# Moving split work, the row norms and the expert offsets of layer 0, and taking layer 1's row norm as factors

## The chip, the cores and the metric

The kernel runs on one core of a Trainium2 chip. The metric is device time in microseconds (us) of one execution. TensorE multiplies matrices, VectorE and ScalarE work on rows and on PSUM results, POOL (GpSimd) prepares the weights, and SyncE issues the DMA transfers. TensorE's granted clock has two levels, 1.2 and 2.4 GHz; the profile writes it as a share of full speed.

## The reference

One graph of 1250 nodes (512 values each) and 20000 edges goes through four layers. What the change touches is the end of layer 0's mixer, layer 0's experts, and layer 1:

```
# layer 0, depth i of 2 (end of it)
y = layernorm(x); h = gelu(y @ W1[i] + b1[i]); x = x + h @ W2[i] + b2[i]
# layer 0, experts, on xf = layernorm(x): two of eight by gate
y = einsum('te,teh->th', combine, relu(xf @ w1 + b1) @ w2 + b2)   # b2: the offsets
x = x + y + relu(xf @ sw1 + sb1) @ sw2 + sb2                      # shared expert
# layer 1, on xn = layernorm(x)
h = (segment_sum(xn[src], dst) / count) @ W_l.T + b_l + xn @ W_r.T
gnn = relu(batchnorm_over_nodes(h)) + xn
z = xn / max(norm(xn), 1e-12) * norm_w * sqrt(512)                # row norm
q, k, v = split(z @ w_qkv); q = softmax over head dims, k = softmax over nodes
x = x + gnn + rmsnorm(attention(q, k, v) @ w_out + b_out)
```

## The kernel before

The 1250 rows are ten tiles t of 125 rows, in three chunks CH of 4, 4 and 2 tiles; the 512 columns are four groups k of 128. A product takes the activations transposed, as a pair of 16-bit halves (high and low), and the weights likewise as a pair, in three passes: `gemm_N` (line 498) gives rows in ten PSUM banks of 12 matmuls, `gemm_T` (line 480) gives transposed results in twelve banks of 12 matmuls, eight of 500 columns and four of 250. PSUM has three rings: "act" (three banks, emptied by ScalarE), "dve" (three, emptied by VectorE) and "both" (two).

**Weights.** A unit is one 512x512 weight. There are two unit slots in SBUF. SyncE loads a unit in four quarters through two raw slots; POOL makes each quarter into its halves with three instructions (`split_quarter`: scale at line 2655, high half at 2657, low half at 2659). POOL and SyncE go through the units u in order, written out by hand: before unit u, POOL waits until the product that used unit u-2 has ended; after it come `4 * SPLIT_AFTER[u]` quarters of the later layers' expert weights, which go by four staging slots in `AT` back to memory. After the last of these (`max(SPLIT_AFTER)`, unit 25) SyncE waits for all stores and loads the adjacency, 3.1 MB, back into `AT` (lines 2883 to 2885). Only then does it issue the quarters of the next unit. SyncE also loads bias rows into two slots, and each waits there for its slot.

Units: 0 is layer 0's graph product; 1 to 12 and 13 to 24 are the two depths of the mixer (4 and 16 are the output products, 5 to 12 and 17 to 24 the hidden layer, in four blocks b of `gemm_T` and `gemm_N`); 25 to 28 the eight experts, 29 and 30 the shared expert; 31 and 32 layer 1's W_l and W_r, both used by one product (`bnT`); 33, 34, 35, 36 its q, k, v and output weights.

**Ends of the depths.** In the last block (b = 3) VectorE takes each tile from PSUM into `M` (line 1850), adds the bias row (1853), in depth 1 adds `M` to `X` (2140), and takes the statistics (1793). At depth 0 the norm, the transposes and the halves of the next product (`normed_columns`, `split_columns`) run beside the last tiles; at depth 1 ScalarE's `ln_root(Y)` norms the rows, and TensorE transposes them (line 430), after the last product. Each act bank of transposes is free again when VectorE has made its low half (1837). The first expert product is interrupted after three banks by the gate's logits.

**Offsets.** `expert_biases` transposes the gates (8 rows) and multiplies them with the 32-bit offset rows E0, 8x512, tile by tile (line 885). VectorE adds each result to `X`; then it adds the experts' results (2375), one instruction for a tile of three matmuls.

**Layer 1.** `gather_N("agg")` sums neighbours (line 539, ten tiles; `AT` has to be back), and in its steps dt the transposes of `M` and of the sums are interleaved (1090), copied by ScalarE (1351) and halved by VectorE. After `bnT` VectorE takes the batch statistics over all banks (2409), ScalarE applies them (1656), VectorE adds `M` to `X` (2424), TensorE transposes back (457) and VectorE adds that (1850). ScalarE squares the rows of `M` (1694), VectorE scales them into `Y` (2526), and TensorE transposes them (430); ScalarE and VectorE make the halves. Then `linear_attention(1)`: q product, query softmax on VectorE (2436 to 2452) with ScalarE's exp, transposes of q, k product (ScalarE empties it), column maxima of k (2458), v product.

## Time and profile before

| | |
|---|---|
| median of 3 runs | 3175.11 us (3169.66 to 3175.34) |
| the profiled execution | 3171.26 us, span 3169.5 us |
| TensorE busy | 2704.7 us (85%), granted clock 0.921 |
| VectorE busy | 1708.1 us (54%) |
| ScalarE, POOL busy | 1125.9 us (36%), 1193.4 us (38%) |

Busy time is that of the whole span. A row of a timeline gives start and length in us, the engine, the line, the operation with the shapes out<-in, the count of instructions merged into it, and in brackets the idle time ahead of it with what ended it. In the numbers of matmuls some records may be missing.

### The profile page before, as it was taken

How to read it: one execution, taken by the hardware profiler on the slowest of the kernel's cores; microseconds unless marked ns; L12 is line 12 of the kernel's file. 1: busy time of each engine (PE TensorE's matmuls, PEld its weight loads, DVE VectorE, ACT ScalarE, POOL GpSimd, SP SyncE). 2: the span in 40 equal slices, each digit the busy share in tenths (PEclk: the TensorE clock that was granted, in tenths of full speed). 3: DMA queues.
4: the chain of work that ended last, by engine and by line, in shares of the span. 5: the costliest groups of instructions: out<-in, count | busy, mean ns of one | idle time of the engine just before them, and what ended most of it. 6: DMA issues, size and time to landing. Idle time of an engine off the chain costs nothing. (4 is left out here: it accounts for less than half of the span.)

```text
span 3169.5 us, 46348 instructions
## 1 busy us (share of the span) xinstructions
PE 2704.7 (85%) x17011; PEld 1760.6 (56%) x17011; DVE 1708.1 (54%) x3454; ACT 1125.9 (36%) x2510; POOL 1193.4 (38%) x1445
## 2 busy tenths in 40 slices
PE   8999899799889889899986956999599958589784
PEld 4655668456558646455544635777355645355453
DVE  8875878434678833655527253222435466541543
ACT  3254466233447522313214323444332235320132
POOL 2031677885377788623212212111003226300042
PEclk9999899999999999989997977999799979798887
DMA  2011445442154444411100007999601059600198
GB/s 63 1 51 37 126 144 160 139 130 80 47 153 147 153 134 131 136 33 34 37 11 27 31 15 286 416 417 414 200 4 38 21 210 322 211 14 0 33 365 271
DMA packets 163941, 415.35 MB, mean 131 GB/s; under 512 B 23931, under 2 KB 75675, under 8 KB 140236
## 3 DMA queue, kind: packets, MB, share of 16 engines
q1 hardware_dynamic: 149213, 362.10, 33.6%
q0 software_dynamic: 12960, 42.48, 3.5%
q10 hardware_dynamic: 1555, 7.95, 1.0%
q8 instruction: 132, 2.16, 0.3%
q14 instruction: 81, 0.66, 0.1%
HBM read 325.37 MB, written 87.09 MB: 130 GB/s over the span
## 5 line engine op out<-in xcount | busy, mean ns | idle before, releaser
L2655 POOL TENSOR_SCALAR raw<-raw 128x512 f32<-128x512 f32 x380 | 271.6, 715 | 1085.8 <-PE ps L480 434.7
L498 PE MATMUL ps<-units,ARENA 128*125 128x512 f16 x2880 | 643.9, 385 | 35.0 <-POOL units L2659 25.6
L480 PE MATMUL ps<-ARENA,units 128*128 128x500 f16 (+1 forms) x2952 | 537.5, 344 | 19.6 <-ACT tmp L1415 9.4
L498 PEld LDWEIGHTS ps<-units,ARENA 128*125 128x125 f16 x2880 | 391.1, 138 | 274.6 <-POOL units L2659 26.1
L480 PEld LDWEIGHTS ps<-ARENA,units 128*128 128x128 f16 x2952 | 289.2, 98 | 265.6 <-issue 19.0
L1813 DVE TENSOR_TENSOR ARENA<-tmp,ARENA 128x500 f16<-128x500 f32 (+3 forms) x241 | 173.1, 723 | 360.8 <-ACT ARENA L1341 187.6
L2659 POOL TENSOR_TENSOR AT<-raw,AT 128x512 f16<-128x512 f32 x200 | 243.9, 1220 | 17.0
L1340 ACT ACTIVATE tmp<-ps,cols 128x500 f32<-128x500 f32 (+1 forms) x156 | 95.7, 613 | 395.1 <-PE ps L480 385.3
L2703 POOL DMA_INDIRECT ARENA<-rows_d,proj x81 | 80.0, 987 | 389.0 <-DVE ARENA L2200 363.0
L2659 POOL TENSOR_TENSOR units<-raw,units 128x512 f16<-128x512 f32 x180 | 217.6, 1209 | 15.3
L2708 POOL DMA_INDIRECT picks_d<-ARENA,proj x81 | 82.1, 1014 | 345.1 <-DVE ARENA L2240 344.5
L973 PE MATMUL ps<-ARENA 128*128 128x128 f16 x3240 | 191.7, 220 | 0.1
L973 PEld LDWEIGHTS ps<-ARENA 128*128 128x128 f16 x3240 | 187.4, 98 | 1.5 <-DVE ARENA L2231 0.6
L988 PE MATMUL ps<-ARENA 128*128 128x512 f16 x810 | 184.2, 380 | 0.0
L1850 DVE SCALAR_TENSOR_TENSOR ARENA<-ps,ARENA 125x512 f32<-125x512 f32 x100 | 68.7, 687 | 153.6 <-PE ps L498 153.4
L430 PE MATMUL ps<-ident,ARENA 125*128 125x125 f32 x280 | 53.1, 352 | 111.8 <-DVE ARENA L1837 33.5
L1594 ACT ACTIVATE tmp<-ps,proj 128x128 f32<-128x128 f32 x270 | 102.6, 380 | 102.8 <-PE ps L973 72.7
L2657 POOL CAST AT<-raw 128x512 f16<-128x512 f32 x200 | 132.9, 664 | 12.8
L613 PE MATMUL ps<-ARENA 125*125 125x500 f16 (+1 forms) x588 | 118.6, 353 | 10.9 <-DVE ARENA L1915 9.9
L988 PEld LDWEIGHTS ps<-ARENA 128*128 128x128 f16 x810 | 74.8, 98 | 95.1 <-issue 12.2
L2240 DVE TENSOR_SCALAR ARENA<-ps,proj 128x512 f32<-128x512 f32 x81 | 60.7, 750 | 121.0 <-PE ps L988 76.9
L655 PE MATMUL ps<-proj,ARENA 128*125 128x256 f16 x640 | 106.0, 296 | 22.3 <-ACT AT L1526 11.4
(445 smaller groups left out, 4578.2 us busy)
## 6 DMA issues: line engine op xcount, KB each, us to landing
ARENA<-split_d SPq DMA_DIRECT2D x135, 1024.0 KB, 11.6
raw<-in_moe SPq DMA_DIRECT2D x200, 256.0 KB, 3.0
split_d<-AT SPq DMA_DIRECT2D x200, 256.0 KB, 2.5
raw<-in_units SPq DMA_DIRECT2D x180, 256.0 KB, 2.5
ARENA<-split_d SPq DMA_DIRECT2D x27, 1280.0 KB, 8.9
rows_d<-ARENA SPq DMA_DIRECT2D x6, 896.0 KB
ARENA<-picks_d SPq DMA_DIRECT2D x6, 896.0 KB
ARENA<-picks_d ACTq DMA_DIRECT2D x6, 896.0 KB
```

Source lines behind the costliest of these rows:

```text
L480: ins = pe.matmul(o[:, 0:nt * R], wt, mv_, start=(i == 0), stop=(i == len(steps) - 1))
L498: ins = pe.matmul(o[0:R, :], th(srcT, h, k, t, 1), w(k, g), start=(i == 0), stop=(i == len(steps) - 1))
L613: ins = pe.matmul(psA[b][0:R, 0:a1 - a0], ohd[j][:, 0:R], ohs[j][:, a0:a1], start=False, stop=False)
L655: ins = pe.matmul(o[0:R, h2 * NBF:(h2 + 1) * NBF], stack(2 * hp + h2, t, 1), features(dep, part), start=(part == 0), stop=(part == 1))
L973: ins = pe.matmul(o[:, oc * B:(oc + 1) * B], w1[:, gw, kk, oc * 128:(oc + 1) * 128], tile_T[g % 2][:, h, kk, :], start=(i == 0), stop=(i = ...
L988: ins = pe.matmul(o[:, :], tile_H[(g - 1) % 2][:, h, b * KC + kk, :], w2[:, gw, kk, :], start=False, stop=(b == halves - 1 and i == len(st ...
L1340: act.activation(tmp[:, i % STAGES, 0:width], o[:, 0:width], func, bias=bias, scale=scale)
L1594: act.activation(tmp[:, i % STAGES, oc * B:(oc + 1) * B], o[:, oc * B:(oc + 1) * B], func, bias=bias, scale=WS)
L1813: tt(lo, tmp[:, staged[0] % STAGES, 0:width], hi, ALU.subtract).then_inc(sem("lo_T"), s.one("lo_T"))
L2655: pool.tensor_scalar(r, r, WEIGHT_SCALE, 1.0, ALU.mult, ALU.mult).then_inc(sem("pool_step"), 1)
L2657: pool.tensor_copy(hi, r).then_inc(sem("pool_step"), 1)
L2659: pool.tensor_tensor(lo, r, hi, ALU.subtract).then_inc(sem(name), 1)
```

## The change

- `SPLIT_AFTER`: units 4, 5, 16, 17 are followed by 32 quarters of expert weights instead of 36; units 26, 27, 28, 29 by 4 each instead of none. The adjacency comes back after unit 29 instead of 25.
- Last blocks of both depths: the bias row is added in block 2 (and in depth 1 `M` is then added to `X`); block 3 adds its products directly to `M` (depth 0) or `X` (depth 1), followed by the statistics alone.
- Depth 1's row norm: the first chunk's transposes go ahead of tile 8 of the last product, the second's and third's behind it, with the copies and low halves interleaved on ScalarE and VectorE.
- Offsets: gates and offsets as 16-bit parts, stacked in 72 rows (high at 0 and 32/64, low), so each tile is one 72x512 16-bit matmul. New copies on VectorE (`offsets_in_parts`, and four instructions in `gates`).
- Layer 1: `M`'s squares are taken by ScalarE at the start of the gather; the norm becomes a factor per row, `row_scale`, applied in q's exp and in v's evacuation, and as a row vector over the columns (`token_scale`, from ten small matmuls with `ones`) in k's evacuation, which VectorE now does. `L1nw` is folded into units 33 to 35 by POOL. The q, k, v products read the transposed `xn` that `bnT` used. `bnT` goes to `M` in transposed form, its statistics are taken bank by bank, its affine step runs between q's exps, and its transposes come after k and q's transposes. The sums X + M move into the gather's steps.

```diff
-SPLIT_AFTER = {4: 9, 5: 9, 16: 9, 17: 9}
-SPLIT_AFTER.update({u: 1 for u in [6, 7, 8, 9, 10, 11] + [18, 19, 20, 21, 22, 23, 24, 25]})
+SPLIT_AFTER = {4: 8, 5: 8, 16: 8, 17: 8}
+SPLIT_AFTER.update({u: 1 for u in [6, 7, 8, 9, 10, 11] + [18, 19, 20, 21, 22, 23, 24, 25, 26, 27, 28, 29]})
...
 # TensorE
+            def direct_columns(c):
+                t0, nt = CH[c]
+                pe.wait_ge(sem("normed"), s.more("normed", nt))
+                for k in range(KC):
+                    pe.wait_ge(*left("act"))
+                    o = bank("act", "lo_D")
...
+            def beside_direct(t):
+                if t == 8:
+                    direct_columns(0)
...
-                    pe.matmul(o[0:R, :], combT[:, t * R:(t + 1) * R], row_slots[0:8, ROWS.index(row) % ROW_SLOTS, :], start=True, stop=True).then_inc(sem("filled_dve"), 1)
+                    pe.matmul(o[0:R, :], combT[:, t * R:(t + 1) * R], offset16[:, :], start=True, stop=True).then_inc(sem("filled_dve"), 1)
...
-            transposes_T(lambda t, a, b: nat(Y, t, a, b), "normed", "lo_D")
+            direct_columns(1)
+            direct_columns(2)
             experts(2, 4, biases="E0", gate=0)
...
-            transposes_N(Q, "bn_relu", "gnn", "dve")
+            pe.wait_ge(sem("scale_rows"), s.more("scale_rows", 1))
+            for t0, nt in CH:
+                pe.wait_ge(*left("act"))
+                o = bank("act", "token_scale")
+                for j in range(nt):
+                    ins = pe.matmul(o[:, j * R:(j + 1) * R], ones[0:R, :], scale_rows[:, (t0 + j) * R:(t0 + j + 1) * R], start=True, stop=True)
+                ins.then_inc(sem("filled_act"), 1)
...
                 gemm_N("YT", lambda k, g: w[:, g, k, :], "qsub")
-                transposes_T(lambda t, a, b: nat(Y, t, a, b), "qn", "qT2")
                 gemm_T([(w, "YT", 0)], "kT2")
+                transposes_T(lambda t, a, b: nat(Y, t, a, b), "qn", "qT2")
+                if mem:
+                    transposes_N(M, "bn_relu", "gnn", "dve")
                 gemm_N("YT", lambda k, g: w[:, g, k, :], "v2")
...
-            transposes_T(lambda t, a, b: nat(Y, t, a, b), "y", "yT")
-            pe.wait_ge(sem("lo_T"), s.more("lo_T", 12))
             linear_attention(1)
...
 # ScalarE
-            ln_root(Y)
-            evac_direct("YT")
+            norm_rows(0, X)
+            for c in range(2):
+                evac_direct("YT", groups=(4 * c, 4 * c + 3))
+                norm_rows(c + 1, X)
+                evac_direct("YT", groups=(4 * c + 3, 4 * c + 4))
+            evac_direct("YT", groups=(8, 12))
...
             evac("both", "x_sel", x_sel[0], D, p=SEL)
+            for t in range(T):
+                act.activation(tmp[0:R, 2, :], nat(M, t), ACT.Square, accum_out=small[0:R, 32 + t:33 + t]).then_inc(sem("act_step"), s.one("act_step"))
+                act.wait_ge(*s.latest())
+            roots(T, small[0:R, 32:32 + T], 0.0, p=R)
             evac_direct("YT")
...
-                    act.activation(tmp[0:R, t % 2, :], tmp[0:R, t % 2, :], ACT.Exp, scale=WS)...
+                    act.activation(tmp[0:R, t % 2, :], tmp[0:R, t % 2, :], ACT.Exp, scale=row_scale[:, t:t + 1] if mem else WS)...
+                    if mem and t in (2, 4, 6, 8):
+                        batch_norm(t // 2 - 1)
...
 # VectorE
+                    if b == 2:
+                        add_to(M, "m_ffn", after=offset_rows)
+                        row_free(f"b2{dep}")
+                    elif b == 3:
+                        add_to(X if dep == 1 else M, "m_ffn", after=x_rows if dep == 1 else stream_rows)
+                    else:
+                        add_to(M, "m_ffn")
...
+                    tt(nat(X, t - 1), nat(X, t - 1), nat(M, t - 1), ALU.add).then_inc(sem("dve_step"), s.one("dve_step"))
+                if t == 5:
+                    dve.wait_ge(sem("std"), s.more("std", 1))
+                    inverse_norms()
+                    ts(row_scale, rstd[0:R, :], float(D) ** 0.5 * WS, None, ALU.mult).then_inc(sem("dve_step"), s.one("dve_step"))
...
+                        for t0, nt in CH:
+                            dve.wait_ge(sem("filled_act"), s.more("filled_act"))
+                            tt(tr(K, k, t0, nt), s.bank("act")[:, 0:nt * R], token_scale[:, t0 * R:(t0 + nt) * R], ALU.mult).then_inc(sem("kT2"), s.one("kT2"))
...
+                if mem:
+                    add_to(X, "gnn", scale=1.0)
...
-                    ts(nat(M, t), o[0:R, :], WS, None, ALU.mult).then_inc(sem("v2"), s.one("v2"))
+                    ts(nat(M, t), o[0:R, :], row_scale[:, t:t + 1] if mem else WS, None, ALU.mult).then_inc(sem("v2"), s.one("v2"))
...
 # POOL
-                pool.tensor_scalar(r, r, WEIGHT_SCALE, 1.0, ALU.mult, ALU.mult).then_inc(sem("pool_step"), 1)
+                pool.tensor_scalar(r, r, WEIGHT_SCALE, gain, ALU.mult, ALU.mult).then_inc(sem("pool_step"), 1)
```

## Rows read from the trace of the kernel before

**Rows 1.** The timeline of TensorE: start and length in us, engine, line, operation, [idle before <-releaser].
```profile
605.04 28.88 PE L498 MATMUL ps<-units,ARENA 128*125 128x512 f16 x120 [12.49 <-POOL units L2659]
...
1137.27 29.00 PE L498 MATMUL ps<-units,ARENA 128*125 128x512 f16 x120 [13.09 <-POOL units L2659]
```

**Rows 2.** The windows view, POOL alone: window and length, busy us (instructions), clock, DMA share, GB/s.
```profile
500.00:600.00 100.00, 76.09 (x90) 0.99 0.50 153
...
```

**Rows 3.** POOL's costliest group, 620 to 780 us: busy us, mean ns | idle before, releasers.
```profile
L2655 POOL TENSOR_SCALAR raw<-raw 128x512 f32<-128x512 f32 x47 | 32.2, 685 | 26.1 <-DMA raw<-in_units 9.8 <-PE ps L480 8.4 <-DMA raw<-in_moe 7.7
```

**Rows 4.** End of depth 0: timeline of VectorE (one row), then of TensorE.
```profile
791.64 1.62 DVE L1853 TENSOR_TENSOR ARENA<-ARENA,row_slots 125x512 f32<-125x512 f32 x1
...
800.87 6.92 PE L480 MATMUL ps<-ARENA,units 128*128 128x500 f16 x24 [3.89 <-ACT tmp L1415]
```

**Rows 5.** End of depth 1 and start of the experts: timeline of TensorE.
```profile
1294.07 21.00 PE L498 MATMUL ps<-units,ARENA 128*125 128x512 f16 x96
...
1336.32 5.42 PE L430 MATMUL ps<-ident,ARENA 125*128 125x125 f32 x24 [12.70 <-DVE ARENA L1837]
...
1342.88 7.76 PE L480 MATMUL ps<-ARENA,units 128*128 128x500 f16 x36
...
1358.14 19.65 PE L480 MATMUL ps<-ARENA,units 128*128 128x500 f16 x108 [2.66 <-ACT ARENA L1341]
```

**Rows 6.** The offset products and what follows: TensorE's timeline, last row VectorE's.
```profile
1379.88 15.29 PE L885 MATMUL ps<-row_slots,ARENA 8*125 8x512 f32 x20 [0.80 <-ACT ARENA L1322]
1395.10 28.60 PE L498 MATMUL ps<-units,ARENA 128*125 128x512 f16 x120
...
1404.66 20.10 DVE L2375 SCALAR_TENSOR_TENSOR X<-ps,kmx,X 125x512 f32<-125x512 f32 x30
```

**Rows 7.** The adjacency reload: timelines of POOL, SyncE's DMA issues, POOL, and TensorE.
```profile
1322.66 1.16 POOL L2659 TENSOR_TENSOR AT<-raw,AT 128x512 f16<-128x512 f32 x1
...
1326.38 0.34 SPq L2883 DMA_DIRECT2D AT<-adj_d  x1
...
1345.14 0.62 POOL L2655 TENSOR_SCALAR raw<-raw 128x512 f32<-128x512 f32 x1 [19.06 <-DMA raw<-in_units]
...
1501.63 26.06 PE L498 MATMUL ps<-units,ARENA 128*125 128x512 f16 x120
```

**Rows 8.** Timeline of ScalarE: the layer-1 gather's first copies, and one square of the norm.
```profile
1543.66 1.07 ACT L1351 ACTIVATE ARENA<-ps 128x500 f16<-128x500 f32 x2
1549.38 1.06 ACT L1351 ACTIVATE ARENA<-ps 128x500 f16<-128x500 f32 x2 [4.66 <-PE ps L1090]
...
1681.47 0.61 ACT L1694 ACTIVATE ARENA<-ARENA 125x512 f32<-125x512 f32 x1
```

**Rows 9.** Layer 1 between the two products: timeline of TensorE.
```profile
1674.06 5.74 PE L457 MATMUL ps<-ident,ARENA 128*125 128x128 f32 x28 [3.75 <-DVE X L1850]
...
1703.29 27.61 PE L498 MATMUL ps<-units,ARENA 128*125 128x512 f16 x120 [1.93 <-DVE ARENA L1813]
...
1738.38 5.93 PE L430 MATMUL ps<-ident,ARENA 125*128 125x125 f32 x28 [6.20 <-ACT ARENA L1322]
1744.20 25.54 PE L480 MATMUL ps<-ARENA,units 128*128 128x500 f16 x144
1769.58 26.06 PE L498 MATMUL ps<-units,ARENA 128*125 128x512 f16 x120
```

**Rows 10.** Timeline of POOL: the weight units of layer 1's queries and keys.
```profile
1653.01 0.62 POOL L2655 TENSOR_SCALAR raw<-raw 128x512 f32<-128x512 f32 x1 [88.78 <-PE ps L480]
...
1663.49 1.05 POOL L2655 TENSOR_SCALAR raw<-raw 128x512 f32<-128x512 f32 x1
```

**Rows 11.** Timeline of VectorE in layer 1: residual sums, the query softmax's first and last step.
```profile
1661.83 11.45 DVE L2424 TENSOR_TENSOR X<-X,ARENA 125x512 f32<-125x512 f32 x10
...
1707.63 0.69 DVE L2436 TENSOR_REDUCE small<-ps 125x8 f32<-125x512 f32 x1 [4.39 <-PE ps L498]
...
1741.14 0.69 DVE L2452 TENSOR_TENSOR ARENA<-tmp,small 125x512 f32<-125x512 f32 x1
```

More of the change, by code:

```diff
@@ L81 @@
 SEL = 9
+PART_ROWS = 72
 MAX16 = 2048
@@ L818, in _ @@
                     else:
-                        gemm_N("Q", lambda k, g: w[:, g, k, :], "m_ffn", by_chunk=True, between=beside_tiles if b == 3 and dep == 0 else None)
+                        gemm_N("Q", lambda k, g: w[:, g, k, :], "m_ffn", by_chunk=True, between=beside_tiles if b == 3 and dep == 0 else beside_direct if b == 3 else None)
                     free(u, "dve")
@@ L1648, in _, with batch_norm @@
             evac("both", "x_sel", x_sel[0], D, p=SEL)
+            for t in range(T):
+                act.activation(tmp[0:R, 2, :], nat(M, t), ACT.Square, accum_out=small[0:R, 32 + t:33 + t]).then_inc(sem("act_step"), s.one("act_step"))
+                act.wait_ge(*s.latest())
+            roots(T, small[0:R, 32:32 + T], 0.0, p=R)
             evac_direct("YT")
             evac_direct("K")
-            evac_T(Q, "bnT", bias=lambda k: col("L1bl", k))
+            evac_T(M, "bnT", bias=lambda k: col("L1bl", k))
+            for t0, nt in CH:
+                evac("act", "token_scale", token_scale[:, t0 * R:(t0 + nt) * R], nt * R)
             act.wait_ge(sem("bn_mv"), s.more("bn_mv", 1))
             roots(KC, mv[:, 0:KC, 1], EPS_LN)
-            act.wait_ge(sem("bn_affine"), s.more("bn_affine", 1))
-            for k in range(KC):
-                act.activation(Q[:, k * N:(k + 1) * N], Q[:, k * N:(k + 1) * N], ACT.Relu,
-                                      bias=colsT[:, 4 + k:5 + k], scale=colsT[:, k:k + 1]).then_inc(sem("bn_relu"), s.one("bn_relu"))
+            def batch_norm(k):
+                if k == 0:
+                    act.wait_ge(sem("bn_affine"), s.more("bn_affine", 1))
+                act.activation(M[:, k * N:(k + 1) * N], M[:, k * N:(k + 1) * N], ACT.Relu,
+                               bias=colsT[:, 4 + k:5 + k], scale=colsT[:, k:k + 1]).then_inc(sem("bn_relu"), s.one("bn_relu"))
             def linear_attention(layer):
@@ L1689, in linear_attention @@
                     roots(T, small[0:R, 32:32 + T], 0.0, p=R)
-            act.wait_ge(sem("xn_all"), s.more("xn_all", 1))
-            for t in range(T):
-                ins = act.activation(nat(Y, t), nat(M, t), ACT.Square, accum_out=small[0:R, 32 + t:33 + t])
-            ins.then_inc(sem("act_step"), s.one("act_step"))
-            act.wait_ge(*s.latest())
-            roots(T, small[0:R, 32:32 + T], 0.0, p=R)
-            act.wait_ge(sem("nw_scaled"), s.more("nw_scaled", 1))
-            evac_pair("YT", "yT", scale=lambda k: col("L1nw", k))
             linear_attention(1)
@@ L2389, in _, with inverse_norms @@
             add_to(X, "shared", "L0sb2", after=lambda t: ln_split(X, M, t))
+            def inverse_norms():
+                ts(std[0:R, :], std[0:R, :], 1e-12, None, ALU.max).then_inc(sem("dve_step"), s.one("dve_step"))
+                dve.wait_ge(*s.latest())
+                dve.reciprocal(rstd[0:R, :], std[0:R, :]).then_inc(sem("dve_step"), s.one("dve_step"))
+                dve.wait_ge(*s.latest())
             s.more("filled_both")
@@ L2405, in _ @@
                     low_direct("K", groups=(4 * t - 32, 4 * t - 28))
-            dve.wait_ge(sem("bnT"), s.more("bnT", 12))
+            dve.wait_ge(*s.latest())
+            for t in range(T):
+                ins = ts(scale_rows[:, t * R:(t + 1) * R], ident[0:R, 0:R], row_scale[:, t:t + 1], None, ALU.mult)
+            ins.then_inc(sem("scale_rows"), s.one("scale_rows"))
             for k in range(KC):
                 for c, (t0, nt) in enumerate(CH):
-                    ins = dve.bn_stats(stats[:, k * 3 + c, :], tr(Q, k, t0, nt))
+                    dve.wait_ge(sem("bnT"), s.more("bnT"))
+                    ins = dve.bn_stats(stats[:, k * 3 + c, :], tr(M, k, t0, nt))
             ins.then_inc(sem("dve_step"), s.one("dve_step"))
@@ L2422, in _ @@
             tt(colsT[:, 4:8], col("L1beta", 0, 4), rstd[:, 0:KC], ALU.subtract).then_inc(sem("bn_affine"), s.one("bn_affine"))
-            for t in range(T):
-                tt(nat(X, t), nat(X, t), nat(M, t), ALU.add).then_inc(sem("dve_step"), s.one("dve_step"))
-            dve.wait_ge(*s.latest())
-            add_to(X, "gnn", scale=1.0)
             def linear_attention(layer):
@@ L2512, in linear_attention @@
                     dve.wait_ge(*s.latest())
-            def inverse_norms():
-                ts(std[0:R, :], std[0:R, :], 1e-12, None, ALU.max).then_inc(sem("dve_step"), s.one("dve_step"))
-                dve.wait_ge(*s.latest())
-                dve.reciprocal(rstd[0:R, :], std[0:R, :]).then_inc(sem("dve_step"), s.one("dve_step"))
-                dve.wait_ge(*s.latest())
-            dve.memset(small[0:R, 0:1], 0.0).then_inc(sem("xn_all"), s.one("xn_all"))
-            ts(col("L1nw", 0, 4), col("L1nw", 0, 4), float(D) ** 0.5, None, ALU.mult).then_inc(sem("nw_scaled"), s.one("nw_scaled"))
-            dve.wait_ge(sem("std"), s.more("std", 1))
-            inverse_norms()
-            for t in range(T):
-                ts(nat(Y, t), nat(M, t), rstd[0:R, t:t + 1], None, ALU.mult).then_inc(sem("y"), s.one("y"))
-            low_parts("YT", "yT")
             linear_attention(1)
@@ L2648, in _, with split_quarter @@
             quarter = [0]
-            def split_quarter(hi, lo, name):
+            def split_quarter(hi, lo, name, gain=1.0):
                 q = quarter[0]
```

82 lines of the change are left out of this document (63 added, 19 removed).

## The prediction

> **What bounds the kernel now.** I read the page's busy shares first (TensorE 85%, VectorE 54%), then the 40 slices, then the waits of TensorE and its timeline over the stages that the change touches. TensorE sets the time: it works nearly without a break in the long products, and its pauses add up straight into the span. So each edit is worth what it takes out of or puts into TensorE's timeline. The pauses that matter here are these: twice 12.5 and 13.1 us for POOL in the hidden layers [rows 1]; 3.9 us at the end of depth 0 [rows 4]; 12.7 us between depth 1 and the experts [rows 5]; a slow stretch of 15.3 us in the offsets [rows 6]; and in layer 1 the whole way from the end of `bnT` at 1652.9 [rows 10] to the q product at 1703.3 [rows 9], 50.4 us with only some 20 us of transposes in them. The sum is made against the profiled execution, 3171.26 us (1.8 more than its span of 3169.5; 3.9 under the median of 3175.11, inside the spread of the runs, 5.7).
>
> **1. Split work.** In a crowded stage POOL turns out 30 quarters in 100 us (90 instructions of three a quarter, [rows 2]), 3.3 us each, its loads' waits included. Units 4 and 5 (16 and 17) lose 4 quarters each, so unit 6 (18) is ready 8 x 3.3 = 26 us earlier, against waits of 12.5 and 13.1. Both go. TensorE also came back at its lower clock: 28.9 and 29.0 us for 120 matmuls that take 26.06 warm [rows 1, 9], 2.8 each. Together 25.6 + 5.7 = 31.3. What is late next is the same splitting a unit later; there POOL already kept up, with 26 us idle in 160 [rows 3], partly for slots. Ends: 22 (part of the relief reappears) to 33. Term: -31.
>
> The 16 quarters go behind units 26 to 29. A unit there takes POOL 10.5 us (1653.0 to 1663.5, [rows 10]) and now 4 x 3.3 = 13 more, 24 in all, against the 26 us that a unit's product lasts: hidden, but for the last. After unit 29's quarters SyncE waits for the stores, issues the reload and only then unit 30's quarters. The before trace has the same sequence at unit 25: last low half ends at 1323.8, the reload is issued at 1326.4, the next unit's first quarter is touched at 1345.1 [rows 7], done 10.5 later: 31.8 us. It starts now 10.5 + 13 after unit 27's product, so unit 30 is ready at 55.3 after it; TensorE wants it after a `gemm_N` and a `gemm_T`, 26.1 + 25.5 = 51.6 [rows 9]. A new wait of some 3 us. Ends: 0 (expert rows run slower, [rows 6]) and 8 (lower clock behind it). The gather comes 26 us later still [rows 7], so the adjacency itself is in time. Term: +3.
>
> **2. Ends of the depths.** Without the bias add, the last tiles of depth 0 cost VectorE 0.7 to 1.6 us less each (one took 1.62 beside POOL, [rows 4]), three tiles behind the catch-up at tile 7: 3.9 us. The chain behind it reaches TensorE as the 3.89 us wait at 800.87 [rows 4]. Ends 0 and 6; term -4. In block 2 the adds are hidden: VectorE has 2.6 us a tile, and its ring lets TensorE run three banks ahead.
>
> At depth 1 tile 7's product ends at 1294.07 + 21.00 = 1315.07 and the first expert product starts at 1342.88 [rows 5]: 27.8 us. In the new order, from the end of tile 7: three transposed banks 1.5; the fourth waits for a low half, which VectorE makes only after tile 7's statistics, ScalarE's root and the reciprocal (4 x 0.7, then 0.7), so at 3.9, done 4.4; tiles 8 and 9 to 9.6. Then VectorE: add, statistics, root, reciprocal to 12.6, first low half 13.3; ScalarE's two norms to 14.1; eight banks of transposes, spaced by low halves of 0.7 each, to 16.4. Product at 16.5: -11.3. Ends -6 (VectorE and ScalarE find each other less neatly) and -14; term -11. The gates' pause of 2.66 [rows 5] stays.
>
> **3. Offsets.** Ten 32-bit tiles take 15.29 us [rows 6]. One pass of 512 columns at 16 bits is below VectorE's 0.67 us a tile (20.1/30, [rows 6]), so VectorE sets the pace: 10 x 0.72 = 7.2. Gain 8. The expert products behind it stay at VectorE's pace. The new copies (an estimate from VectorE's small instructions, 0.2 to 0.7 each, seven of them, 3 us) lie under the 7.76 us of the first product's three banks and the gates. Ends -5 and -10; term -8.
>
> Here a rule speaks against the change. Two-input VectorE work in SBUF takes 1.145 us instead of 0.69 while POOL splits (11.45 for ten, [rows 11], against [rows 6]'s 0.67 with PSUM as one input). The Trainium skill, SBUF — State Buffer, section "Who interferes with whom", says that an instruction with two SBUF inputs contends with a GpSimd instruction that reads SBUF, and one with at most one does not. The experts' sums have one tensor in SBUF and one in PSUM. By the rule the moved quarters cost them nothing, which is the row's reading too; were the rule wrong for them, 80 sums x 0.45 = 36 us would come back (a rival below).
>
> **4. The gather of layer 1.** ScalarE takes ten squares before its first copy. One is 0.61 us [rows 8]; with the read-out of its sum and, new, a wait for its own end I estimate 0.88, 8.8 in all, from 1543.7 (when the first copy ran before) to 1552.6. Three act banks are free, so the fourth transposed group, copied at about 1549.9 [rows 8], has to wait for the first low half at 1554: 4.7 us. The sums X + M, one a step, fit into VectorE's slack; the last tile's costs 0.8 at the end. Ends 0 and 9; term +5.5.
>
> **5. Layer 1's norm as factors.** Before: from `bnT`'s end 1652.9 [rows 10] to the end of the v product, 1769.58 + 26.06 = 1795.6 [rows 9]: 142.7. After:
> - unit 33 can't be split before `bnT` lets go of its slot: 10.5 us [rows 10]. This wait was hidden; now it is what comes last. The token factors (ten small matmuls, 2 to 3 us) lie in it. A scale from a column instead of a constant may cost POOL 0 to 0.5 us a quarter; no row shows one.
> - q product at the lower clock at first: 28.8 [rows 1].
> - VectorE's softmax ends at 1741.14 + 0.69, 38.5 after q's start at 1703.29 [rows 9, 11]. The k product fills three banks by 35.2 and waits for VectorE's first multiplication at 39.3. k ends at 6.4 + 4.1 + 19.1 = 29.6 after q's end.
> - q's transposes: 28 in 5.93 [rows 9] and 12 into free banks, some 2: 7.9; `bnT`'s transposes back: 28 in 5.74 [rows 9], 40 in 8.2, paced by VectorE's adds 8.8; v 26.1.
>
> Sum 10.5 + 28.8 + 29.6 + 7.9 + 8.8 + 26.1 = 111.7. Gain 31. ScalarE's four affine steps fit between exps, which stand over 3 us apart (34 us for ten tiles, [rows 11]). The maxima and exps of k lie under the transposes and v. Ends -20 (another low-clock product, VectorE late for k) and -38; term -31.
>
> **Sum.** -31 + 3 - 4 - 11 - 8 + 5.5 - 31 = -76.5. 3171.3 - 76.5 = 3094.8; I say 3096, leaning a little to the side on which hidden costs lie.
>
> **Rivals.**
> - *The split work isn't relieved.* POOL sets the pace of the whole hidden layer (8 quarters of 3.3 a unit are 26 us against TensorE's 26), so the 26 us come back unit by unit. For it: that near-equality. Against it: POOL's 26 us idle [rows 3]. Time 3096 + 31 = 3127.
> - *Contention in the experts* as priced in 3: 3096 + 36 = 3132. Against it: line 1850 and 2375 at 0.67 to 0.69.
> - *Layer 1 stays VectorE's.* If the softmax, the k multiplications and the maxima run slower than I lay them out, or the q weights come 5 us late, the gain there is 16: 3111.
> - *Slower than before: the reload.* Unit 30 hangs on POOL's last quarter, the stores, 3.1 MB and the loads behind them. It costs what exceeds 28 us from the last low half. The kernel is slower than before only if this chain, 31.8 us in the row, took 110. With 120 us it ends at 3181. Nothing in the trace points there.
>
> **How the numbers follow.** Forecast 0.66 (3080 to 3108 by the terms' ends, which don't all fall together), layer 1 smaller 0.17, split work or contention 0.11, larger gains than mine (3070) 0.03, the reload 0.02 slower and 0.01 with nothing left of the gain. The range takes in the forecast, the smaller layer 1 and part of the third: 3078 to 3122. What can be told from no change here is 0.2%, 6 us: faster 0.97, same 0.01, slower 0.02.
>
> **What would show it.** No wait of TensorE for POOL at units 6 and 18, but one of 8 to 10 us behind `bnT`, and one of 0 to 8 ahead of unit 30. L885 at 0.7 us a tile. A pause of some 4 us in the gather's second step, on VectorE behind ScalarE. One of about 4 us in k's fourth bank. The expert product 16 to 19 us after tile 7. `bnT` to the end of v near 112 us. I am wrong if a POOL wait shows again in units 7 to 12, if line 2375 exceeds 0.7 us, or if layer 1 keeps a pause over 12 us.

## The result, and the profile after

The changed kernel takes 3087.72 us (median of 4 runs, 3084.43 to 3097.36) against 3172.39 us for the kernel before in the same session (3166.62 to 3175.34): ratio 0.974, 95% interval 0.9713 to 0.9767. The prediction was 3096, range 3078 to 3122. A second set of five runs, in a later session, gave 0.9751 [0.9722, 0.978], with a median of 3098.3 and a wider spread (3086.89 to 3108.95). The first session's profiled execution took 3084.43 us, span 3082.7, granted clock 0.931 (0.921 before): 86.8 us less than the profiled execution before.

All rows in this section are of the changed kernel's timeline, with the columns of the rows of before. Its line numbers moved: L522 is `gemm_N` (498 before), L504 `gemm_T` (480), L461 the transposes of the two row norms' ends, L438 the other transposes to columns, L481 those back to rows, L2743 POOL's low half (2659).

TensorE at units 6 and 18, which answers to [rows 1]:

```profile
594.39 26.06 PE L522 MATMUL ps<-units,ARENA 128*125 128x512 f16 x120
...
1107.01 26.06 PE L522 MATMUL ps<-units,ARENA 128*125 128x512 f16 x120
```

Both waits for POOL are gone, and so is the slow start behind each (28.9 and 29.0 us before, at a granted clock of 0.50 in the first 5 us).

TensorE at the end of depth 0 and at the end of depth 1, which answers to [rows 4, 5]:

```profile
783.97 2.71 PE L504 MATMUL ps<-ARENA,units 128*128 128x500 f16 x12 [0.46 <-ACT tmp L1447]
...
1285.36 0.65 PE L461 MATMUL ps<-ident,ARENA 125*128 125x125 f32 x4 [2.33 <-DVE ARENA L1880]
1285.84 5.34 PE L522 MATMUL ps<-units,ARENA 128*125 128x512 f16 x24
...
1294.46 0.80 PE L461 MATMUL ps<-ident,ARENA 125*128 125x125 f32 x4 [2.00 <-DVE ARENA L1880]
1295.43 2.49 PE L461 MATMUL ps<-ident,ARENA 125*128 125x125 f32 x8 [0.17 <-ACT ARENA L1436]
1297.71 9.71 PE L504 MATMUL ps<-ARENA,units 128*128 128x500 f16 x36
```

One wait of 12.7 us has become two of 2.33 and 2.00. From the end of tile 7 (1260.86 + 20.88) the first expert product starts 16.0 us later, 27.8 before. But its first three banks take 9.71 us instead of 7.76. The granted clock is 0.50 from 1296 to 1300 us and 0.59 in the next 2, so this product starts at the lower level; before, it was the transposes behind the long wait that started at 0.50, and the product began at 1.00.

TensorE's offset products and the experts' first row product, against [rows 6]:

```profile
1336.93 0.86 PE L908 MATMUL ps<-ARENA 72*125 72x512 f16 x3 [0.80 <-ACT ARENA L1354]
...
1339.34 3.08 PE L908 MATMUL ps<-ARENA 72*125 72x512 f16 x5 [0.17 <-DVE X L1893]
1342.42 3.90 PE L522 MATMUL ps<-units,ARENA 128*125 128x512 f16 x9
```

The ten tiles take 5.5 us instead of 15.3; behind the first three each waits 0.2 to 0.4 us for VectorE to free a bank. The reload, POOL's first quarter behind it and the product of unit 30, against [rows 7]:

```profile
1417.08 1.16 POOL L2743 TENSOR_TENSOR AT<-raw,AT 128x512 f16<-128x512 f32 x1
...
1420.80 0.34 SPq L2969 DMA_DIRECT2D AT<-adj_d  x1
...
1438.94 0.62 POOL L2739 TENSOR_SCALAR raw<-raw 128x512 f32<-128x512 f32 x1 [20.70 <-DMA raw<-in_units]
...
1450.29 26.11 PE L522 MATMUL ps<-units,ARENA 128*125 128x512 f16 x120 [1.40 <-POOL units L2743]
```

The chain last low half to unit ready is 32.0 us (31.8 before); a wait of 1.4 us is what TensorE sees of it. Then the gather: the first of ScalarE's ten squares with its read-out (the next starts at 1492.13), its first copies, and TensorE's pause in the second step, against [rows 8].

```profile
1491.39 0.61 ACT L1686 ACTIVATE tmp<-ARENA 125x512 f32<-125x512 f32 x1
1491.91 0.18 ACT L1686 ACTIVATION_READ_ACCUMULATOR tmp<-ARENA 125x1 f32 x1
...
1499.03 1.52 ACT L1383 ACTIVATE ARENA<-ps 128x500 f16<-128x500 f32 x3
...
1500.43 1.10 PE L1114 MATMUL ps<-ident,ARENA 125*128 125x125 f32 x4 [3.27 <-DVE ARENA L1880]
```

TensorE in layer 1 from `bnT` to the value product, against [rows 9]:

```profile
1554.51 52.46 PE L504 MATMUL ps<-ARENA,units 128*128 128x500 f16 x288
1606.81 2.40 PE L1145 MATMUL ps<-AT,ones 125*128 125x125 f32 x20
...
1617.56 28.54 PE L522 MATMUL ps<-units,ARENA 128*125 128x512 f16 x120 [8.35 <-POOL units L2743]
1645.93 6.51 PE L504 MATMUL ps<-ARENA,units 128*128 128x500 f16 x36
1657.62 22.07 PE L504 MATMUL ps<-ARENA,units 128*128 128x500 f16 x108 [5.18 <-DVE ARENA L2550]
1679.53 5.33 PE L438 MATMUL ps<-ident,ARENA 125*128 125x125 f32 x40
1684.70 5.67 PE L481 MATMUL ps<-ident,ARENA 128*125 128x128 f32 x40
1690.36 26.08 PE L522 MATMUL ps<-units,ARENA 128*125 128x512 f16 x120
```

Two waits are left, each where it was placed: for POOL at the query weights, and for VectorE (L2550, the key banks' multiplication) in the key product's fourth bank.

One thing was not in the prediction. `linear_attention` is also layer 2's, and there too the query transposes now come behind the key product. TensorE in layer 2, before:

```profile
2423.36 1.45 PE L430 MATMUL ps<-ident,ARENA 125*128 125x125 f32 x12
2429.25 5.39 PE L430 MATMUL ps<-ident,ARENA 125*128 125x125 f32 x28 [4.45 <-ACT ARENA L1322]
```

and after:

```profile
2345.43 25.55 PE L504 MATMUL ps<-ARENA,units 128*128 128x500 f16 x144
2370.82 5.33 PE L438 MATMUL ps<-ident,ARENA 125*128 125x125 f32 x40
```

A bank of transposes had waited there for ScalarE's copies. With the key product between, the softmax is done when they come: 6.1 us less.

**Where the time went.** A checkpoint is the start of the same product in both timelines. This is how far TensorE's checkpoints moved from one profiled execution to the other, term by term:

| step | predicted | measured |
|---|---|---|
| split work, units 6 and 18 | -31 | -13.5 - 15.7 = -29.2 |
| new wait at unit 30 | +3 | +1.4 |
| end of depth 0 | -4 | -4.0 |
| end of depth 1 | -11 | -12.0 |
| expert product's first three banks, gates' pause (3.07, was 2.66) | 0 | +2.1 |
| offsets | -8 | -9.6 |
| layer 1's gather | +5.5 | +5.7 |
| layer 1, `bnT` to the end of v | -31 | -33.6 |
| sum | -76.5 | -79.2 |
| layer 2's order | not seen | -6.1 |
| the rest | | -1.5 |

The split work's -29.2 is known to some 3 us only: the changed kernel's execution was already 2.0 us behind in the hidden product of unit 5, ahead of the first wait, and the other executions stand there from 0.4 ahead to 3.6 behind the kernel before. Counted from that product on, the term is -31.2.

### The profile page after: what moved, and what is told of

Read it like the earlier page. It is cut to its first block and busy times, and to the rows that moved or that the text cites. A ratio compares the mean times of both kernels' runs of the same rounds, so it can differ in the third digit from the quotient of the medians.

```text
span 3082.7 us, 46251 instructions
## 1 busy us (share of the span) xinstructions
PE 2687.0 (87%) x16981; PEld 1746.4 (57%) x16981; DVE 1705.9 (55%) x3462; ACT 1106.4 (36%) x2477; POOL 1196.3 (39%) x1445
## 5 line engine op out<-in xcount | busy, mean ns | idle before, releaser
L522 PE MATMUL ps<-units,ARENA 128*125 128x512 f16 x2880 | 640.7, 384 | 15.5 <-POOL units L2743 9.8
L2739 POOL TENSOR_SCALAR raw<-raw 128x512 f32<-128x512 f32 x368 | 258.8, 703 | 885.6 <-PE ps L504 331.4
L504 PE MATMUL ps<-ARENA,units 128*128 128x500 f16 (+1 forms) x2952 | 544.8, 347 | 22.6 <-ACT tmp L1447 6.0
L522 PEld LDWEIGHTS ps<-units,ARENA 128*125 128x125 f16 x2880 | 389.9, 138 | 251.4 <-DVE X L2450 16.5
L504 PEld LDWEIGHTS ps<-ARENA,units 128*128 128x128 f16 x2952 | 291.6, 99 | 273.9 <-issue 27.2
L1856 DVE TENSOR_TENSOR ARENA<-tmp,ARENA 128x500 f16<-128x500 f32 (+3 forms) x229 | 161.4, 710 | 368.6 <-ACT ARENA L1373 182.7
L2743 POOL TENSOR_TENSOR AT<-raw,AT 128x512 f16<-128x512 f32 x200 | 242.3, 1211 | 17.0
L2743 POOL TENSOR_TENSOR units<-raw,units 128x512 f16<-128x512 f32 x180 | 219.6, 1220 | 15.3
L1372 ACT ACTIVATE tmp<-ps,cols 128x500 f32<-128x500 f32 (+1 forms) x144 | 87.6, 608 | 355.1 <-PE ps L504 348.1
L2741 POOL CAST units<-raw 128x512 f16<-128x512 f32 x180 | 124.6, 692 | 11.5
L1011 PEld LDWEIGHTS ps<-ARENA 128*128 128x128 f16 x810 | 74.8, 98 | 95.1 <-issue 12.2
L1383 ACT ACTIVATE ARENA<-ps 128x500 f16<-128x500 f32 (+1 forms) x156 | 75.0, 516 | 121.3 <-PE ps L1114 58.3
```

The costliest lines, as they stand in the source:

```text
L504: ins = pe.matmul(o[:, 0:nt * R], wt, mv_, start=(i == 0), stop=(i == len(steps) - 1))
L522: ins = pe.matmul(o[0:R, :], th(srcT, h, k, t, 1), w(k, g), start=(i == 0), stop=(i == len(steps) - 1))
L1011: ins = pe.matmul(o[:, :], tile_H[(g - 1) % 2][:, h, b * KC + kk, :], w2[:, gw, kk, :], start=False, stop=(b == halves - 1 and i == len(st ...
L1856: tt(lo, tmp[:, staged[0] % STAGES, 0:width], hi, ALU.subtract).then_inc(sem("lo_T"), s.one("lo_T"))
L2739: pool.tensor_scalar(r, r, WEIGHT_SCALE, gain, ALU.mult, ALU.mult).then_inc(sem("pool_step"), 1)
L2741: pool.tensor_copy(hi, r).then_inc(sem("pool_step"), 1)
```

## The experiments

Times of a variant are compared by its timeline, from one checkpoint to the next, because single executions of the changed kernel lie up to 24 us apart. The medians stand beside. A warm product is one that runs at the full clock throughout.

**Split work back.** The changed kernel with the old `SPLIT_AFTER`.

```diff
-SPLIT_AFTER = {4: 8, 5: 8, 16: 8, 17: 8}     # and 1 each after units 26 to 29
+SPLIT_AFTER = {4: 9, 5: 9, 16: 9, 17: 9}
```

> The changed kernel with the old distribution of split work (9, 9, 9, 9 and nothing behind units 26 to 29), the rest as changed. Theory (POOL was late for units 6 and 18, and only the 26 us of relief moved): TensorE waits for POOL again some 12 and 13 us at the second product of the hidden layer, with about 2.8 us of lower clock behind each; the 1.4 us wait ahead of unit 30 goes; time +28 us against the changed kernel (ratio to the kernel before about 0.983). Rival (the waits went because the other parts gave POOL or its loads air): waits under 5 us each, time within 10 us of the changed kernel.

Median 3120.29 (3114.62 to 3126.65), ratio 0.9844 [0.9824, 0.9864]: 32.6 above the changed kernel's first median. TensorE's timeline has both waits again:

```profile
603.71 27.93 PE L522 MATMUL ps<-units,ARENA 128*125 128x512 f16 x120 [11.19 <-POOL units L2743]
...
1130.28 27.47 PE L522 MATMUL ps<-units,ARENA 128*125 128x512 f16 x120 [13.11 <-POOL units L2743]
```

Unit 18's product ends at 1157.6 instead of 1132.9 (+24.7), and no wait stands ahead of unit 30. The move alone makes the term (26.7, counted from unit 5's hidden product on). The median says 32.6; what exceeds the timeline isn't explained and lies inside the spread of the executions.

**Split work alone.** The kernel before with only that edit.

> The kernel before with one edit: the new distribution of the expert weights' split work (8 instead of 9 after units 4, 5, 16, 17; 1 more after units 26 to 29), all else as before. My theory: additive, as the reverse edit in the changed kernel said (24.7 us on TensorE's timeline at the end of unit 18, and the extra wait at unit 30). Expected -26 to -30 against the kernel before: both POOL waits (12.5 and 13.1 us) gone, products 26.1 instead of 29, and a wait of some 1 to 4 us ahead of unit 30. Rival: the new order at the ends of the depths is needed for the relief (it shifts when the slots come free); then a wait for POOL is left at unit 18 and the gain is under 20.

Median 3145.98 (3140.22 to 3156.6) against 3174.09, ratio 0.9907 [0.9889, 0.9924]: -28.1. The end of unit 18's product moves by -29.8 (1136.3 against 1166.1; -33.4 from unit 5's hidden product on), and the wait at unit 30 is 3.4 us, again as foretold:

```profile
1110.39 26.06 PE L498 MATMUL ps<-units,ARENA 128*125 128x512 f16 x120
...
1476.71 13.55 PE L498 MATMUL ps<-units,ARENA 128*125 128x512 f16 x54 [3.40 <-POOL units L2659]
```

So the edit is additive: it needs none of the others. The first rival (the 26 us return unit by unit) falls in both directions.

**Offsets at 32 bits again.** Products, transposes and gates' parts as before the change; a single execution.

```diff
-    pe.matmul(o[0:R, :], combT[:, ...], offset16[:, :], ...)
+    pe.matmul(o[0:R, :], combT[:, ...], row_slots[0:8, ...], ...)
```

> The changed kernel with the 32-bit offsets of before (8 rows of gates against 8 rows of offsets, no parts). Theory (TensorE's 32-bit passes at the lower clock paced the stage): the ten tiles take 15.3 us again instead of 5.5, from the transposes of the gates to the first expert rows +9 to 10 us, the rest unchanged. Rival (VectorE's adds pace it, and the stage gained from elsewhere): under 4 us.

From the expert product's fourth bank to the experts' first row product it is 36.95 us (1317.47 to 1354.42) against 27.35: +9.6, all of it in the ten tiles, and the same size as the gain. The profiled time is 3107.13.

```profile
1339.59 14.90 PE L909 MATMUL ps<-row_slots,ARENA 8*125 8x512 f32 x20 [0.80 <-ACT ARENA L1355]
```

**Bias rows back in block 3.** In depth 1 the sum of `M` into `X` goes back with them; the transposes stay interleaved. A single execution.

```diff
-                    if b == 2:
-                        add_to(M, "m_ffn", after=offset_rows)
+                    if b == 3:    # product, bias row, (M to X in depth 1), statistics
+                        add_to(M, "m_ffn", after=x_rows if dep == 1 else m_rows)
```

> The changed kernel with the bias rows added again in the last hidden block of both depths (block 3), and the product added to M first in depth 1, then M to X; transposes and norms stay interleaved as changed. My theory: at depth 0 the old wait of some 3.9 us ahead of the next depth's first product is back (+3 to +5). At depth 1 the chain from tile 7 to the first expert product, 17 us now, grows by two VectorE instructions a tile for three tiles and their waits: +3 to +8. The rest unchanged. Sum +6 to +13. Rival: depth 1's gain came from the interleaving alone and VectorE has slack there: +4 in all.

Depth 0: the wait of 3.89 us is back (+3.5). Depth 1: 28.7 us from tile 7 to the experts instead of 16.0, +12.7, outside the range that I gave. That is the old order's 27.8 again: the interleaving is worth nothing without the moved adds. The reverse, moved adds without the interleaving, was not run, so how the 12 us divide is not shown. The timelines of this variant show where it waits, first TensorE ahead of tile 8, then VectorE. TensorE's tile 7 had ended at 1280.2.

```profile
1291.65 1.09 PE L461 MATMUL ps<-ident,ARENA 125*128 125x125 f32 x4 [10.13 <-DVE ARENA L1880]
...
1281.16 1.53 DVE L2185 TENSOR_TENSOR X<-X,ARENA 125x512 f32<-125x512 f32 x1
1282.73 0.69 DVE L1836 BATCH_NORM_STATS2 stats<-X 125x6 f32<-125x512 f32 x1
1283.34 0.67 DVE L1893 SCALAR_TENSOR_TENSOR ARENA<-ps,ARENA 125x512 f32<-125x512 f32 x1
1284.05 1.58 DVE L2182 TENSOR_TENSOR ARENA<-ARENA,row_slots 125x512 f32<-125x512 f32 x1
...
1289.16 0.69 DVE L1836 BATCH_NORM_STATS2 stats<-X 125x6 f32<-125x512 f32 x1
```

With four instructions a tile VectorE has next to no idle time and is two tiles behind: tile 7's statistics start at 1289.2, at 1282.5 in the changed kernel, where VectorE waits 1.17 us for TensorE in between. L2182 and L2185 read two tensors in SBUF and stretch to 1.58 us beside POOL, while L1893, with PSUM as an input, stays at 0.67 to 0.69. VectorE takes 3.15 us a tile (1265.29 to 1268.44 to 1271.59) against TensorE's 2.6; I had counted two short ones a tile for three tiles and missed the backlog of the tiles before. In all this execution took 3112.12, 27.7 us over the first profiled one, of which 14.9 had arisen by the start of `bnT`. Layer 1 and layer 2 add nothing (13.8 at layer 2's output product); the last 13.9 lie behind it. The two profiled executions of the unaltered changed kernel differ there by 9.0, so I take most of them for chance, which is not shown.

**Squares between the copies.** ScalarE takes two squares after every two copies instead of ten ahead.

```diff
-            for t in range(T):
-                act.activation(tmp[0:R, 2, :], nat(M, t), ACT.Square, ...)
-            evac_direct("YT")
+            for i in range(5):
+                evac_direct("YT", groups=(2 * i, 2 * i + 2))
+                for t in (2 * i, 2 * i + 1): act.activation(...)   # as above
+            evac_direct("YT", groups=(10, 12))
```

> The changed kernel with ScalarE's ten squares set between the first ten copies of the layer-1 gather, two behind each pair, instead of all ahead of them. Theory (the squares hold the first copy, so VectorE's first low half, so the fourth act bank): TensorE's wait of 3.3 us in the gather's second step goes, and so do the 2.5 us of lower clock behind it; the gather is 5 to 6 us shorter. Rival (VectorE's added sums X + M make the gather longer): the gather stays within 1.5 us of the changed kernel's.

The 3.27 us wait goes, and the steps run at 4.53 us each from the first one. From the start of unit 30's product to `bnT` it is 99.8 us against 104.2, with that product 1.7 us slower here, so about 6 us less in the gather: the whole of the +5.7 was the ten squares ahead of the first copy. The median, 3086.12 (ratio 0.9727 [0.9711, 0.9743]), can't be told from the changed kernel's.

**Layer 2 in the old order.** A single execution.

```diff
+                if not mem:
+                    transposes_T(lambda t, a, b: nat(Y, t, a, b), "qn", "qT2")
                 gemm_T([(w, "YT", 0)], "kT2")
```

> The changed kernel with the old order in layer 2 alone: the query transposes between the query product and the key product. Theory (the order was changed in both layers, and layer 2 gained the 6 us that the prediction did not have): the wait of some 4.5 us for ScalarE comes back in layer 2's query transposes and the stage from the query product to the value product is 6 us longer. Rival (the 6 us are spread of the runs): the stage stays within 1.5 us.

TensorE waits again, and the layer's projections take 6.5 us longer (168.8 against 162.3):

```profile
2356.98 5.81 PE L438 MATMUL ps<-ident,ARENA 125*128 125x125 f32 x28 [4.43 <-ACT ARENA L1357]
```

**Query weights into a free arena.** Unit 33's halves go to `Q`, so POOL need not wait until `bnT` has ended.

```diff
-                slot = units[:, u % UNIT_SLOTS, :]
+                slot = Q[:, 0:KC * D] if u == 33 else units[:, u % UNIT_SLOTS, :]
...
-                        name, value = unit_release[u - UNIT_SLOTS]
+                        name, value = unit_release[30 if u == 33 else u - UNIT_SLOTS]
```

> The changed kernel with one edit: the halves of layer 1's query weights (unit 33) go into the arena Q, free at that time, instead of the unit slot that bnT holds, so POOL can split them during the gather. My theory: the 8.35 us wait of TensorE for POOL behind bnT (itself followed by a 28.54 us query product, 2.5 over the warm 26.05) is a plain wait for a slot. It should go, and the query product run at 26.1; VectorE's softmax then starts 9 us earlier, but is paced by itself (3.8 us a tile), so TensorE's pause in the key product grows from 5.2 to some 6.8. Expected: faster than the changed kernel by 9.5 to 10.5 us. Rival: something else holds the query product (VectorE's low halves or the token factors), and the wait stays with another releaser: 0 to 2 us gained. Second rival: POOL's splitting of unit 33 beside the gather slows VectorE there, and 2 to 4 us come back.

```profile
1562.31 51.54 PE L504 MATMUL ps<-ARENA,units 128*128 128x500 f16 x288
1615.92 26.07 PE L522 MATMUL ps<-ARENA 128*125 128x512 f16 x120
...
1653.24 22.10 PE L504 MATMUL ps<-ARENA,units 128*128 128x500 f16 x108 [4.92 <-DVE ARENA L2550]
1686.01 26.09 PE L522 MATMUL ps<-units,ARENA 128*125 128x512 f16 x120
```

The wait and the slow product are gone, `bnT` to v is 123.7 us instead of 135.9: -12.2, or -10.4 against the changed kernel's second profiled execution (134.1). The wait was one for a slot. The pause in the keys did not grow (4.92), so that part of my expectation was wrong. The softmax still takes 34 us, but VectorE gets its first bank 2.8 us after the product's start instead of 5.3: the warm product saves its 2.5 us ahead of the first tile, and VectorE gains them too. The median, 3083.26 (ratio 0.9719 [0.9703, 0.9735]), shows 4.5 of the gain, and its interval overlaps the changed kernel's; `bnT` here started 7.8 us later than in the first profile, 6 of that before unit 29's product.

**Key banks emptied by ScalarE.** VectorE multiplies the factors in from SBUF, one instruction of 1250 columns ahead of each group's maxima.

```diff
-    for t0, nt in CH:
-        tt(tr(K, k, t0, nt), s.bank("act")[:, 0:nt * R], token_scale[...], ALU.mult)
+    tt(K[:, k * N:(k + 1) * N], K[:, k * N:(k + 1) * N], token_scale[:, :], ALU.mult)
```

> The changed kernel with layer 1's key banks emptied by ScalarE again (scale 1), and the token factors multiplied in by VectorE in SBUF, four instructions of 1250 columns, one ahead of each group's column maxima. My theory: the 5.2 us pause of TensorE in the key product's fourth bank is VectorE, which is still at the query softmax when the first three banks are full; ScalarE is free there. The pause and the lower clock behind it (22.07 for 108 matmuls) go, -5 to -8 us, and the maxima and exps of k come up to 4 us later, hidden under the transposes back and the value product. Rival: ScalarE is busy with the query exps and the copies of q, so the pause stays with ScalarE as releaser: 0 to -2. Second rival: VectorE, late by the multiplications, delays what stands behind the value product: +3 to +6 there.

```profile
1658.51 19.21 PE L504 MATMUL ps<-ARENA,units 128*128 128x500 f16 x108 [1.40 <-ACT ARENA L1354]
```

Against the changed kernel's second profiled execution, on the same chip, the pause is 1.40 instead of 4.96, the banks behind it take 19.2 us instead of 21.9, and `bnT` to v is 127.9 instead of 134.1: -6.2. The stage behind v is unchanged (56.3 us from v to the next row product in both). The medians are 3086.08 and 3098.3, with overlapping intervals (0.9716 [0.9695, 0.9736] and 0.9751 [0.9722, 0.978]), so the timeline's 6.2 is the better figure.

**The reload behind unit 30's quarters.** SyncE issues it at the end of unit 30's turn instead of unit 29's; a single execution.

```diff
-                if u == max(SPLIT_AFTER):
+                if u == max(SPLIT_AFTER) + 1:
```

> The changed kernel with the adjacency reload issued by SyncE after unit 30's quarters instead of before. My theory: the 1.40 us wait of TensorE ahead of unit 30's product, which POOL ends, comes from unit 30's loads standing behind the wait for the stores and the 3.1 MB of the reload; it goes, and the adjacency still arrives ahead of the gather. Expected -1.4 us, within what one look can tell only in the trace: POOL's 20.7 us idle ahead of unit 30's first quarter shrinks to under 10. Rival: POOL's own work sets it, the wait stays. Second rival: the reload now collides with unit 31's loads or comes too late for the gather: a new wait at its start, several us slower.

Unit 30's wait is gone, but the second rival decides the run: 3114.97.

```profile
1508.70 6.82 PE L563 MATMUL ps<-AT 125*125 125x512 f16 x20 [33.89 <-DMA AT<-adj_d]
```

SyncE's own timeline tells how:

```profile
1419.33 10.16 SPq L2928 DMA_DIRECT2D raw<-in_units  x3
1485.06 0.28 SPq L2861 DMA_DIRECT2D row_slots<-in_rows  x1
1485.53 0.31 SPq L2969 DMA_DIRECT2D AT<-adj_d  x1
```

The queue also holds a bias-row load, which waits until its slot comes free at 1485.1. I had moved the reload behind it. So it was issued again ahead of the row load:

> The changed kernel with the adjacency reload issued by SyncE after unit 30's quarters again, but ahead of the bias-row load that stood in front of it in the run before last's edit (there the reload was issued only at 1485.5, behind a row load that waited for its slot, and the gather waited 33.9 us for it). My theory: the position in SyncE's queue against the row load was the whole damage, and unit 30's wait for POOL comes from standing behind stores and reload. Expected: reload issued at about 1430 and back by 1460, no DMA wait at the gather (1476), no POOL wait ahead of unit 30: -1.4 to -3.4 us against the changed kernel, little against its spread of runs; the trace decides. Rival: 3.1 MB beside unit 31's loads and the gather's start delay one of them: a wait of a few us at the gather or ahead of bnT.

It now goes out at 1435.4, the gather waits for no DMA, and unit 30's product starts warm:

```profile
1429.03 25.55 PE L504 MATMUL ps<-ARENA,units 128*128 128x500 f16 x144
1454.41 26.06 PE L522 MATMUL ps<-units,ARENA 128*125 128x512 f16 x120
```

From unit 29's product to `bnT` it is 129.5 us against 133.1 on the same chip: -3.6. The median, 3091.25 (0.9729 [0.9709, 0.975]), can't show that.

**The changed kernel again, and the four edits together** (squares, query weights, reload ahead of the row load, key banks).

> The changed kernel itself, unaltered, on the same chip as the other three, to compare with. Expected: ratio to the kernel before of 0.973 to 0.974, as measured first. Where one look of a variant stood further from it than its stage explains (the single look of the bias edit: 24 us in all, 15 of them by the start of layer 1's product), its own spread of runs shows how much of that is chance.

> The changed kernel with the four edits together: squares two by two between the gather's copies, query weights' halves in a free arena, reload behind unit 30's quarters and ahead of the row load, key banks emptied by ScalarE. Theory, by TensorE's timeline of the single edits: squares -4 to -6, query weights -9.5 to -12, reload -1.4 to -3, keys -5 to -8; with the query product earlier VectorE stays its own pace, so the keys' pause would have grown and is removed whole. Expected -21 to -27 against the changed kernel in the same runs. Rival: the gains overlap, since layer 1 from bnT on is then bound by VectorE (query softmax, then k maxima), which shows as a new wait of TensorE in q's transposes or ahead of the attention products: -12 to -16.

| | median (range), 5 runs each | ratio to before |
|---|---|---|
| changed kernel | 3098.30 (3086.89 to 3108.95) | 0.9751 [0.9722, 0.978] |
| with the four edits | 3077.57 (3066.24 to 3080.39) | 0.9684 [0.9662, 0.9706] |

TensorE of the combined kernel in layer 1:

```profile
1544.94 52.45 PE L504 MATMUL ps<-ARENA,units 128*128 128x500 f16 x288
...
1599.45 26.07 PE L522 MATMUL ps<-ARENA 128*125 128x512 f16 x120
1625.36 6.51 PE L504 MATMUL ps<-ARENA,units 128*128 128x500 f16 x36
1633.28 19.21 PE L504 MATMUL ps<-ARENA,units 128*128 128x500 f16 x108 [1.42 <-ACT ARENA L1354]
...
1663.16 7.09 PE L522 MATMUL ps<-units,ARENA 128*125 128x512 f16 x32
```

From unit 29's product to the value product the two executions of this chip differ by 24.8 us (242.4 against 267.2): 2.8 at unit 30, 6.2 in the gather, 15.8 in layer 1. The single edits, against the same execution or (the squares) the first one, sum to 26.2: 3.6 for the first two stages without the squares, 6, and 10.4 + 6.2. So 1.4 is lost by overlap or chance, and no new wait took their place. The medians say 20.7, and the intervals of the ratios don't touch: this version beats both kernels.

## Why the prediction was right, step by step

**Split work** held, by its own working: a backlog of 26 us against waits of 12.5 and 13.1 that both vanish, with the slow start behind them. -29.2, -29.8 alone, and 24.7 when undone in the changed kernel, against 31.3, all inside 22 to 33; counted from unit 5's hidden product on they are 31.2, 33.4 and 26.7, so the close match is in part luck. Its row on POOL was read too narrowly: the 26 us [rows 3] are the idle time ahead of the scaling alone. All of POOL's is 39.6 of 160 us (busy 120.4), which speaks against the rival more strongly still. The waits that I had called late next (units 7 to 12) never showed.

**The reload chain** held to 0.2 us (32.0 us, predicted from 31.8), and the wait at unit 30 (1.4 in the first profile, 2.4 to 3.4 in others) was inside 0 to 8. What I didn't see is that the row load in the same queue makes the place of the reload a matter of 34 us, which only the failed variant showed. The prediction's slow case also has a slip: by its own rule a chain of 120 us costs 92, which ends near 3184 and not at 3181.

**Ends of the depths.** -4.0 and -12.0 against -4 and -11, and the product starts 16.0 us after tile 7 where 16.5 was laid out. Two points behind it were missed: the expert product's first banks at the lower clock (+2.0), and how much of the gain hangs on the bias (12.7, not a share of it). Right in size, so, with a cause wider than I had it: the adds in block 2 take VectorE out of a backlog. That the interleaving then uses it is argued, since no run has one without the other.

**Offsets.** "VectorE sets the pace, 10 x 0.72" was pessimistic: three banks are in hand and only seven tiles are paced (5.5 us instead of 7.2), and VectorE's last additions run beside the row product's first matmuls.

**Contention in the experts** did not come. The experts' sums (L2450, 80 of them) take 53.6 us busy, mean 743 ns, against 53.6 and 742 before, although POOL is now busy for 63.5 of 108 us beside them instead of 31.0 of 107. (Neighbours overlap a little: 53.6 / 80 is the 0.67 us of the prediction, whose limit of 0.7 is meant so.) The halves of the hidden layers (L1856, two tensors in SBUF) did stretch, from 654 to 712 ns on average, and cost nothing, since VectorE waits there for ScalarE. The Trainium skill's rule (SBUF — State Buffer, "Who interferes with whom") agrees here on both sides: the sums have one input in SBUF, and the instructions with two (L1856 here, L2182 and L2185 in the bias variant, up to 1.58 us) are those that stretched.

**The gather** was +5.7 for +5.5, with errors that cancel: a square costs 0.75 us with its read-out, not 0.88, so the wait is 3.27, not 4.7; what makes it up is the lower clock behind it (0.64 granted), 7.04 us for the next step's 20 matmuls instead of 4.53.

**Layer 1** was -33.6 for -31. Query weights: the product starts 10.8 us after `bnT`'s end (predicted 10.5), then 28.5 (28.8). Keys: a pause of 5.2 instead of 4.1, and 22.1 for nine banks instead of 19.1, again the clock. The surplus gain is in the two transpose groups: 5.3 and 5.7 us, where 7.9 and 8.8 were taken. I had paced them by VectorE's and ScalarE's rows of the old order, where these engines were still at earlier work. Layer 2 shows this for q's transposes: 28 of them take 5.81 us behind a wait in the old order, all 40 take 5.33 in the new. "Layer 1 stays VectorE's" had its symptom (the fourth bank) but not its size. No run takes the factors themselves back, so this term, the largest, rests on the two timelines; the variants test only the two waits that it leaves.

**What failed** is a reading of the diff: the step "q's transposes behind k" was priced for layer 1 only, though the function serves two layers. Like with like, the sum's 3094.8 stands against the profiled execution's 3084.43: the 10.3 between them are 2.7 in the terms, 6.1 here and 1.5 in the rest. The median is 8.3 under the forecast of 3096, and the second session's is 2.3 over it, so the error in sight is no larger than the spread between sessions.

## What to carry to other kernels

When work is moved off the engine that supplies the bottleneck, count the backlog in units of work times the supplier's pace, compare it with the sum of the waits, and look whether the supplier idles later: both were in the trace of before, and gave 31 where 29 was measured. Before a transfer is moved in a queue, list every entry that it is moved past with the time at which each can go: one row load turned an expected 1.4 us gain into a wait of 34 us. And list every caller of a function in which an order is changed.

## What the runs showed of the hardware that was not expected

- A short wait of TensorE costs more than itself, and not in proportion. Unit 30's product, 120 matmuls, took 26.06 us without a wait ahead and 26.11 behind 1.40 us, but 27.80 behind 2.38 and behind 2.64. Behind the 2.38 us the granted clock is 0.78 of full speed from 1455 to 1460 us and 0.88 in the next 5, so partly at the lower level (1.2 GHz); behind the 1.40 us it is 1.00 throughout. So a wait of 2.4 us was a loss of 4.1. In all eight executions with a wait of 2.38 to 3.40 us ahead of this product it took 27.7 to 27.8.
- Executions of the changed kernel spread over 24 us (3084.43 to 3108.95, nine runs in two sessions). Between its two profiled executions (14.1 us apart), 5.1 us had arisen by the second depth's unit 18 and another 9 in and behind layer 2. An edit worth 2 to 6 us is to be read in the timeline of its stage.
